# One root of a product in place of two nested roots in a hyperbolic attention, with work moved between VectorE, ScalarE and GpSimd

## The chip, the cores and the metric

The kernel runs on one core of one Trainium2 chip. The metric is the time of one execution on the device, in microseconds (us); the median of several executions is compared. PE is TensorE, DVE is VectorE, ACT is ScalarE, POOL is GpSimd, SP is SyncE.

## What is computed

The reference is one layer of a perceiver. All inputs are float32, and x has 2 batches of 256 tokens with 256 channels. Three blocks follow each other, each with a residual sum: a softmax cross attention of 16 heads to 4096 context tokens a batch, a self attention of 16 heads of 16 channels with a hyperbolic distance, and a feed-forward block of 8 experts of which each token takes the one with the highest gate. The change touches the second block only:

```
diff_sq = q_norm_sq + k_norm_sq - 2.0 * qk
denom = maximum((1.0 - q_norm_sq) * (1.0 - k_norm_sq), 1e-06)
dist = arccosh(maximum(1.0 + 2.0 * diff_sq / denom, 1.0))
attn = softmax(-dist, axis=-1)
out = einsum('bhnm,bhmd->bhnd', attn, v)
```

With r = max(diff_sq, 0) / denom, exp(-dist) can be had in two ways. The kernel before forms sqrt(2r) + sqrt(2r + 2), takes the logarithm and raises e to -2 times it. The kernel after forms sqrt(r * (r + 1)) + r, takes the logarithm of 4 times it plus 2, and raises e to -1 times it. Both give half of exp(-dist); the factor falls out of the softmax.

## The kernel before, in words

The cross attention comes first: 16 steps (8 pairs of heads by 2 batches), each over the 4096 keys. It takes most of the time. The last step (`last_step`) already has batch 0 of the second block in it: its projections, its lengths, and its 16 distance units, which DVE turns into ratios.

**The units.** The second block has 32 units m, 16 a batch, in 8 groups gg of 4 (groups 0 to 3 are batch 0, 4 to 7 are batch 1). A unit is 128 keys by 256 queries of two heads; PE leaves numerator and reciprocal denominator in two banks of PSUM (`distances`, L659 and L663), and a group is a tile of 128x2048 float32. `ratios` (L1134, L1136) has two DVE instructions a unit: the maximum with zero of the numerators, 128x512, into the group's tile, and a `scalar_tensor_tensor` that multiplies it by the smaller of 1e6 and the other half of the banks. Each batch has two pairs of banks, so PE may begin unit m only when DVE has counted up `s_rt` for unit m - 2.

**From ratios to weights.** For each group ACT takes two square roots (`root_of_product` L929 into a tile of its own, `root_of_sum` L932 in place), POOL adds them for groups 0 to 5 (L527) and DVE for 6 and 7 (L1199), ACT takes the logarithm (L944) and the exponential (L949), and PE multiplies the weights with the values (`average`, L735). Root, logarithm and exponential each need a table that is loaded when the function changes (ACT_TABLE_LOAD).

**The order after the cross attention.** It is written out by hand, an engine at a time, in `tail_dve`, `tail_act`, `tail_pe` and `tail_pool`. DVE takes the last output of the cross attention from PSUM (`take_output`, L1986), normalises it, PE turns it, ACT copies it (`take_turned_output`, L1754), PE projects it, and DVE adds it to x (`add_output`, L2004). Then come the layer norm of batch 1 (`variance`, `root_of_variance` L859, `normalised`) and its transposition (`take_batch`, L573). Then eight projections of batch 1 go round PE (`qk`, `lengths`, `norms`), ACT (`squares` L887, `rows` L896) and DVE (`low_rows` L1083), in three banks. After each, ACT's program may have one of the large operations of batch 0. Then DVE has 11 small instructions in a chain for the denominators (`inverses`, L1092 to L1108), PE places them, and ACT and DVE copy four groups each (`take_placed` L909, `take_placed_keys` L1116). Then come batch 1's 16 units, u = 0 to 15. Between them PE has the averages and turned averages of batch 0 (AVERAGE_AFTER) and turns and projects batch 0's output (`turn_output` L672, `project_output` L685), ACT copies the averages out (`take_average` L969) and the turned output (L973), and DVE has `normalise(0)` (L1183, L1187) after unit 12. DVE then adds batch 0's residual (`residual`, L1144), and the layer norm of batch 0 follows, with ACT's root L859 ahead of the logarithms and exponentials of groups 4 to 7. The experts come last.

**What waits.** An engine works through its own list in order; a wait stops all that stands behind it. In the list of ACT before, between the last rows and the layer norm of batch 0, stand in this order: logarithms 0 and 1, values 1, logarithm 2, four placed copies, logarithm 3, weights 0 to 2, average 0, weights 3, average 1, roots of group 4 with averages 2 and 3 between and behind, roots of 5 and 6, the turned output, roots of 7.

Of the kernel before, what the change touches and what calls it, by code (L numbers as in the profile page):

```python
# [20 lines left out]
ALU = mybir.AluOpType  # L21
# [69 lines left out]
BEHIND = 3  # L91
AVERAGE_AFTER = {4: (0, None), 6: (1, 0), 8: (2, 1), 9: (3, 2), 11: (None, 3)}
# [15 lines left out]
def perceiver(nc, x, ctx, wq, wk, wv, wo, aq, ak, av, ao, gw, gb, w1, b1, w2, b2, out):  # L108
# [8 lines left out]
    with stack:  # L117
# [213 lines left out]
        s_r2 = sem("s_r2")  # L331
        s_ra = sem("s_ra")
# [9 lines left out]
        s_rb = sem("s_rb")  # L342
# [175 lines left out]
        def tail_pool(pool):  # L518
# [393 lines left out]
        def tail_act(act, take_turned_output):  # L912
# [6 lines left out]

            def root_of_product(gg):  # L920

                act.wait_ge(s_rt, 8 * (gg + 1))
                if gg == 1:
                    act.wait_ge(s_el, 8)
                if gg == 2:
                    act.wait_ge(s_pv, STEPS * SLOTS)
                if gg >= 4:
                    act.wait_ge(s_ra, gg - 2)
# [6 lines left out]
            def roots(gg):  # L935
                root_of_product(gg)
                root_of_sum(gg)

            def logarithms(gg):
                if gg < 6:  # L940
                    act.wait_ge(s_ra, gg + 1)
                else:
                    act.wait_ge(s_rb, gg - 5)
                nc.scalar.activation(ratio[gg], ratio[gg], ACT.Ln).then_inc(s_lg, 1)  # L944

            def weights(gg):

                act.wait_ge(s_lg, gg + 1)
                nc.scalar.activation(ratio[gg], ratio[gg], ACT.Exp, scale=-2.0).then_inc(s_wt, 1)  # L949
# [1234 lines left out]
```

## Time and profile before

| what | value |
|---|---|
| median of 3 executions | 1107.04 us (1106.72 to 1108.7) |
| the profiled execution, its own time | 1108.32 us |
| span of the profiled execution | 1106.6 us |
| busy share of PE, DVE, ACT, POOL | 94%, 70%, 71%, 60% |
| mean granted clock of TensorE | 0.974 |
| end of PE's last matmul of the cross attention | 955.57 us of the span |

The span runs from the first to the last instruction; 1.72 us of the execution's own time lie around it. Shares are means over the whole span. A granted clock of 1.00 is full speed, 2.4 GHz, and 0.50 is 1.2 GHz. Idle time in a row is that just ahead of the instruction, and the arrow names what ended it. "xN" at a row of the timeline is N instructions merged.

### The profile page before, as it was taken

The page shows a single profiled execution, that of the slowest core. Times are in us where ns is not written, and L with a number is a line of the kernel's source. Part 1 is how long each engine was busy: PE and PEld are TensorE (multiplying, and loading weights), DVE is VectorE, ACT ScalarE, POOL GpSimd, SP SyncE. Part 2 cuts the span into 40 slices and gives each one's busy share as a digit, 9 for nine tenths or more (in the row PEclk, how much of TensorE's full clock was granted, in tenths as well). Part 3 has the DMA queues.
Part 4 walks back from the last instruction along what each step waited for, and adds up shares of the span by engine and source line. Part 5 has one row for each costly group of instructions (what it writes and reads, how often), then busy time and mean ns, then how long its engine had stood idle before and what let it go on. Part 6 is the DMA issues. An engine that isn't in the chain of part 4 may idle for free.

```text
span 1106.6 us, 36226 instructions
## 1 busy us (share of the span) xinstructions
PE 1041.5 (94%) x15401; PEld 778.4 (70%) x15401; DVE 773.8 (70%) x1061; ACT 783.3 (71%) x1197; POOL 667.0 (60%) x611
## 2 busy tenths in 40 slices
PE   6799999999999999999999999999999989667888
PEld 3376777777777777777777777777777777543566
DVE  4887877777777777777777777777767759558442
ACT  6487777777777777777777777777777756799754
POOL 6366666666666666666666666776655456833033
PEclk9999999999999999999999999999999999886699
DMA  7821330000000000000000000003000020000000
GB/s 225 238 48 26 64 55 7 17 7 16 7 16 7 17 7 16 7 17 7 17 7 17 8 16 7 16 8 121 7 2 7 9 72 3 2 1 1 1 1 20
DMA packets 50929, 31.70 MB, mean 29 GB/s; under 512 B 27194, under 2 KB 47698, under 8 KB 50770
## 3 DMA queue, kind: packets, MB, share of 16 engines
q1 hardware_dynamic: 50770, 29.39, 10.0%
q8 instruction: 123, 2.02, 0.8%
q14 instruction: 36, 0.29, 0.1%
HBM read 22.57 MB, written 0.52 MB: 21 GB/s over the span
## 4 chain that ended last, share of the span: by engine, by line
PE 82%; DVE 5%; ACT 5%; issue 4%; POOL 3%; DMA 1%; ACTq 0%; POOLq 0%; DVEq 0%
PE ps L1461 15%; PE ps L1406 14%; PE ps L1543 14%; PE ps L1490 6%; PE ps L1589 5%; PE ps L1584 5%; PE ps L1587 5%; PE ps L1531 5%; PE ps L815 2%; POOL psums L2151 2%; PE ps L775 2%; PE ps L1522 1%; PE ps L1391 1%; PE ps L591 1%; DVE m_part L1956 1%
## 5 line engine op out<-in xcount | busy, mean ns | idle before, releaser
L2151 POOL TENSOR_TENSOR psums<-probs 128x512 f16<-128x512 f32 x512 | 589.6, 1171 | 327.0 <-ACT probs L1790 270.0
L1956 DVE TENSOR_REDUCE m_part<-ps 128x2 f32<-128x1024 f32 x256 | 312.7, 1223 | 137.3 <-PE ps L1490 135.3
L1781 ACT ACTIVATE probs<-ps 128x1024 f32<-128x1024 f32 x256 | 259.8, 1015 | 200.4 <-PE ps L1543 155.4
L1790 ACT ACTIVATE probs<-probs 128x512 f16<-128x512 f32 x384 | 240.0, 627 | 4.2
L1543 PE MATMUL ps<-q_hi,k_p 64*128 64x256 f16 x2048 | 211.2, 269 | 0.0
L1584 PE MATMUL ps<-v_sb,probs 128*128 128x65 f16 x2048 | 205.1, 192 | 4.9 <-POOL psums L2151 3.6
L1587 PE MATMUL ps<-v_sb,probs 128*128 128x64 f16 x2048 | 205.0, 192 | 0.0
L1589 PE MATMUL ps<-v_sb,psums 128*128 128x65 f16 x2048 | 204.6, 194 | 0.0
L1584 PEld LDWEIGHTS ps<-v_sb,probs 128*128 128x128 f16 x2048 | 188.3, 98 | 20.0 <-POOL psums L2151 5.1
L1587 PEld LDWEIGHTS ps<-v_sb,probs 128*128 128x128 f16 x2048 | 187.9, 97 | 16.1
L1589 PEld LDWEIGHTS ps<-v_sb,psums 128*128 128x128 f16 x2048 | 188.1, 97 | 0.0
L1461 PE MATMUL ps<-wv_hi,ctx_hi 128*128 128x128 f16 x1024 | 179.4, 220 | 1.6 <-DVE v_sb L1971 1.6
L1461 PE MATMUL ps<-wv_lo,ctx_hi 128*128 128x128 f16 x1024 | 178.1, 219 | 0.0
L1461 PE MATMUL ps<-wv_hi,ctx_lo 128*128 128x128 f16 x1024 | 178.1, 219 | 0.0
L1543 PE MATMUL ps<-q_lo,k_p 64*128 64x256 f16 x1024 | 143.0, 269 | 0.0
L1947 DVE TENSOR_TENSOR k_p<-ps,k_p 128x512 f16<-128x512 f32 x124 | 85.7, 691 | 65.1 <-ACT k_p L1741 65.1
L1461 PEld LDWEIGHTS ps<-wv_hi,ctx_hi 128*128 128x128 f16 x1024 | 99.9, 98 | 40.8 <-issue 38.9
L1543 PEld LDWEIGHTS ps<-q_hi,k_p 64*128 64x128 f16 x2048 | 106.3, 94 | 19.2
L1978 DVE CAST probs<-probs 128x512 f16<-128x512 f32 x128 | 115.6, 903 | 1.5 <-ACT probs L1781 1.4
L1490 PE MATMUL ps<-k_p,q_hi 64*128 64x512 f16 x512 | 99.0, 380 | 12.3 <-DVE m_part L1956 7.1
L1531 PE MATMUL ps<-m_row,level 64*128 64x512 f16 x512 | 98.9, 376 | 1.9 <-ACT probs L1781 1.1
L1461 PEld LDWEIGHTS ps<-wv_lo,ctx_hi 128*128 128x128 f16 x1024 | 100.3, 98 | 0.1
(251 smaller groups left out, 1661.2 us busy)
## 6 DMA issues: line engine op xcount, KB each, us to landing
ctx_hi<-in_L_ffn_W_dram SPq DMA_DIRECT2D x2, 2048.0 KB, 10.3
probs<-in_ctx_dram SPq DMA_DIRECT2D x4, 512.0 KB, 7.4
wqk_raw<-in_L_xattn_w_q_dram SPq DMA_DIRECT2D x16, 128.0 KB, 2.3
wqk_raw<-in_L_xattn_w_k_dram SPq DMA_DIRECT2D x16, 128.0 KB, 2.5
k_p<-in_ctx_dram SPq DMA_DIRECT2D x4, 512.0 KB, 10.5
wv_raw<-in_L_xattn_w_v_dram SPq DMA_DIRECT2D x16, 128.0 KB, 2.5
wo_raw<-in_L_xattn_w_o_dram SPq DMA_DIRECT2D x16, 128.0 KB, 2.1
ctx_hi<-in_ctx_dram SPq DMA_DIRECT2D x7, 256.0 KB, 5.8
```

The source lines that it names most:

```text
L1406: mm = pe.matmul(ps[:, bank, :], w[:, par, c, :], y[:, b, j, c, :], start=(c == 0 and i == 0), stop=(c == 1 and i == 2))
L1461: mm = pe.matmul(ps[:, bank, t * P:(t + 1) * P], y[:, b, j, c, toks], w[:, par, c, :], start=(k == 0), stop=(k == 5))
L1490: mm = pe.matmul(ps[:, bank + 1 - h, :], q_hi[rows, n % 3, t * P:(t + 1) * P], k_p[rows, par, 0, 512 * j:512 * (j + 1)], start=True, stop= ...
L1531: pe.matmul(ps[:, score_bank(n, pair, h), :].rearrange("p (k q) -> p k q", k=2), level[rows, :], m_row[rows, n % 2, :].unsqueeze(1).to_bro ...
L1543: mm = pe.matmul(ps[:, score_bank(n, pair, h), cols], k_p[rows, par, k_part, keys], q_part[rows, n % 3, :], start=False, stop=(i == 2), sk ...
L1584: pe.matmul(out, p_hi[:, s % NP, h, queries], value[:, XD:2 * XD + 1], start=(s == 0 and h == 0 and t == 0), stop=False, skip_group_check= ...
L1587: pe.matmul(ps[:, ACC, at:at + XD], p_hi[:, s % NP, h, queries], value[:, 0:XD], start=False, stop=False, skip_group_check=True)
L1589: mm = pe.matmul(out, p_lo[:, s % NP, h, queries], value[:, XD:2 * XD + 1], start=False, stop=(s == SLOTS - 1), skip_group_check=True)
L1781: nc.scalar.activation(p_raw[:, s:s + 2, :, :].rearrange("p k h q -> p h k q"), ps[:, first:first + 2, :].rearrange("p h (k q) -> p h k q" ...
L1790: nc.scalar.activation(p_hi[:, s % NP, :, :], p_raw[:, s % NX, :, :], ACT.Copy) \
L1956: nc.vector.tensor_reduce(m_part[:, j, t, :], ps[:, bank:bank + 2, :], AX.X, ALU.max) \
L2151: nc.gpsimd.tensor_tensor(p_lo[:, s % NP, :, :].rearrange("p h q -> p (h q)"), p_raw[:, s % NX, :, :].rearrange("p h q -> p (h q)"), p_hi[ ...
```

## The change

ACT has one root for each group instead of two. DVE forms its argument, ratio times (ratio plus one), in one `scalar_tensor_tensor` of 128x2048, and adds the root to the ratio for all eight groups; POOL's six sums go. The maximum with zero of batch 1's units moves from DVE to ACT (`positive`, Relu). The logarithm takes scale 4 and a bias from a column, and stands between the rows for groups 0 to 3. Two tables of places, ROOT_AFTER and SUM_AFTER, set where groups 4 to 6 go among batch 1's units; AVERAGE_TAKEN does so for ACT's copies of the averages.

```diff
+AVERAGE_TAKEN = {5: 0, 7: 1, 9: 2, 10: 3}
+ROOT_AFTER = {5: 4, 9: 5, 13: 6}
+SUM_AFTER = {5: 4, 9: 5, 13: 6}
...
-            for gg in range(6):
-                pool.wait_ge(s_r2, gg + 1)
-                nc.gpsimd.tensor_tensor(ratio[gg], root_of(gg), ratio[gg], ALU.add) \
-                    .then_inc(s_ra, 1)
...
+            def positive(m, gg, kt, jj):
+                act.wait_ge(s_dd, m + 1)
+                if gg <= 6:
+                    act.wait_ge(s_pv, STEPS * SLOTS)
+                    act.wait_ge(s_ra, 1)
+                else:
+                    act.wait_ge(s_el, 8)
+                pair = ps[:, UNIT_BANKS[1][jj]:UNIT_BANKS[1][jj] + 2, :]
+                part = head_part(gg, kt, slice(2 * jj, 2 * jj + 2)).rearrange("p (h q) -> p h q", h=2)
+                nc.scalar.activation(part, pair[:, :, 0:TQ], ACT.Relu).then_inc(s_rl, 1)
+
             def root_of_product(gg):
...
-                nc.scalar.activation(root_of(gg), ratio[gg], ACT.Sqrt, scale=2.0)
-
-            def root_of_sum(gg):
-                nc.scalar.activation(ratio[gg], ratio[gg], ACT.Sqrt, scale=2.0,
-                                     bias=vecs[:, 2:3]).then_inc(s_r2, 1)
...
+                act.wait_ge(s_tp, gg + 1)
+                nc.scalar.activation(root_of(gg), root_of(gg), ACT.Sqrt).then_inc(s_r2, 1)
 
             def logarithms(gg):
...
-                nc.scalar.activation(ratio[gg], ratio[gg], ACT.Ln).then_inc(s_lg, 1)
+                act.wait_ge(s_ra, gg + 1)
+                nc.scalar.activation(ratio[gg], ratio[gg], ACT.Ln, scale=4.0,
+                                     bias=vecs[:, 2:3]).then_inc(s_lg, 1)
 
             def weights(gg):
...
-            roots(0)
+            root_of_product(0)
+            root_of_product(1)
             act.wait_ge(s_vone, 2)
             take_turned_output()
-            root_of_product(1)
+            root_of_product(2)
             root_of_variance(act, 2, slice(2, NT))
-            root_of_sum(1)
             take_values(0)
             take_batch(act, 1)
+            root_of_product(3)
             for i in range(9):
                 take_rows(act, i, 1)
-                if i in (1, 3):
-                    root_of_product(2 + i // 2)
-                if i in (2, 4):
-                    root_of_sum(1 + i // 2)
+                if i in (1, 3, 5, 7):
+                    logarithms(i // 2)
...
+            weights(0)
+            weights(1)
             take_values(1)
-            logarithms(2)
+            weights(2)
             for g in range(4):
                 take_placed(act, 1, g)
...
             weights(3)
...
+            for u, (m, gg, b, g, kt, jj) in enumerate(attn_units()[16:]):
+                positive(m, gg, kt, jj)
+                if u in AVERAGE_TAKEN:
+                    take_average(AVERAGE_TAKEN[u])
+                if u in ROOT_AFTER:
+                    root_of_product(ROOT_AFTER[u])
             take_turned(1, 0, OUT_BANKS[0][0])
-            roots(7)
+            root_of_product(7)
             root_of_variance(act, 3, slice(0, 2))
             for gg in range(4, 8):
                 logarithms(gg)
...
+            if b == 1:
+                dve.wait_ge(s_rl, m - 15)
+                nc.vector.scalar_tensor_tensor(part, pair[:, :, TQ:2 * TQ], 1e6, part,
+                                               ALU.min, ALU.mult).then_inc(s_rt, 2)
+                return
...
+        def product(dve, gg):
+            dve.wait_ge(s_rt, 8 * (gg + 1))
...
+            nc.vector.scalar_tensor_tensor(root_of(gg), ratio[gg], 1.0, ratio[gg], ALU.add, ALU.mult) \
+                .then_inc(s_tp, 1)
+
+        def sum_of_roots(dve, gg):
+            dve.wait_ge(s_r2, gg + 1)
+            nc.vector.tensor_tensor(ratio[gg], root_of(gg), ratio[gg], ALU.add).then_inc(s_ra, 1)
...
             variance(2, slice(2, NT))
             normalised(2, slice(2, NT))
+            product(dve, 3)
+            sum_of_roots(dve, 0)
             for i in range(8):
                 low_rows(dve, i, 1)
+                if i in (0, 2, 4):
+                    sum_of_roots(dve, 1 + i // 2)
...
             for u, (m, gg, b, g, kt, jj) in enumerate(attn_units()[16:]):
                 ratios(dve, m, gg, b, kt, jj)
+                if u % 4 == 3:
+                    product(dve, gg)
+                if u in SUM_AFTER:
+                    sum_of_roots(dve, SUM_AFTER[u])
                 if u == NORMALISE_AFTER:
                     normalise(0)
...
-            sum_of_roots(6)
             residual(0)
             variance(3, slice(0, 2))
             normalised(3, slice(0, 2))
-            sum_of_roots(7)
+            sum_of_roots(dve, 7)
...
             last_step(STEPS - 1)
+            for gg in range(2):
+                product(dve, gg)
             take_output(STEPS - 1, STEPS * SLOTS - 1)
             normalise(STEPS - 1)
+            product(dve, 2)
             add_output(STEPS - 1, 1)
```

## Rows read from the trace of the kernel before

**Rows 1.** The page: span and instructions, and the shares of the chain by engine.
```profile
span 1106.6 us, 36226 instructions
...
PE 82%; DVE 5%; ACT 5%; issue 4%; POOL 3%; DMA 1%; ACTq 0%; POOLq 0%; DVEq 0%
```

**Rows 2.** The chain that ended last, 1015 to 1024 us: start, us, what.
```profile
1015.64 0.59 ACT xnT L973
...
1016.27 3.80 PE ps L685 x8
...
1020.09 0.70 DVE x_sb L1144
...
1022.31 1.28 ACT L944
```

**Rows 3.** Busy time by stretch; after POOL the granted clock, DMA share, GB/s.
```profile
950.00:966.00 16.00, 9.88 (x68) 7.10 (x69) 5.87 (x17) 11.84 (x13) 12.04 (x14) 0.68 0.01 2
966.00:982.00 16.00, 14.65 (x66) 11.64 (x65) 3.38 (x7) 13.23 (x20) 11.44 (x3) 1.00 0.00 1
...
993.00:1018.00 25.00, 19.23 (x192) 9.55 (x193) 22.60 (x37) 23.75 (x19) 9.04 (x2) 0.70 0.00 1
```

**Rows 4.** Groups by line, ScalarE, 930 to 1107 us: busy, mean ns, idle before.
```profile
L932 ACT ACTIVATE k_p<-k_p,vecs 128x2048 f32<-128x2048 f32 x4 | 8.0, 1994 | 0.0
L944 ACT ACTIVATE k_p<-k_p 128x2048 f32<-128x2048 f32 x4 | 7.5, 1902 | 0.0
...
L944 ACT ACT_TABLE_LOAD x2 | 2.6, 1283 | 0.0
...
L973 ACT ACTIVATE xnT<-ps 128x512 f32<-128x512 f32 x2 | 1.2, 590 | 1.7 <-PE ps L672 1.7
```

**Rows 5.** Two lines side by side, VectorE and GpSimd: ns min/median/max.
```profile
L880 DVE SCALAR_TENSOR_TENSOR ctx_hi<-ctx_hi x4: 1212/1598/2177, 938.9 to 949.3; 128x1024 f16<-128x1024 f32 x4
...
L2151 POOL TENSOR_TENSOR psums<-probs x14: 1154/1159/2145, 931.4 to 953.5; 128x512 f16<-128x512 f32 x14
```

**Rows 6.** VectorE in order of time: start us, us, instruction, idle before it.
```profile
955.61 0.43 DVE L1986 COPY o_acc<-ps 128x264 f32<-128x264 f32 x1 [4.18 <-PE ps L1589]
...
960.15 0.69 DVE L2004 TENSOR_TENSOR x_sb<-x_sb,ps 128x512 f32<-128x512 f32 x1 [3.44 <-PE ps L1522]
...
982.45 0.41 DVE L1092 TENSOR_SCALAR last_raw<-ps 128x256 f32<-128x256 f32 x1
...
992.99 0.69 DVE L1134 TENSOR_SCALAR v_sb<-ps 128x512 f32<-128x512 f32 x1 [1.17 <-PE ps L663]
...
1012.65 0.76 DVE L1187 TENSOR_TENSOR xn<-ps,orec 128x256 f32<-128x256 f32 x2
...
1016.68 0.69 DVE L1136 SCALAR_TENSOR_TENSOR ctx_hi<-ps,ctx_hi 128x512 f32<-128x512 f32 x1
1017.29 2.28 DVE L1199 TENSOR_TENSOR ctx_lo<-probs,ctx_lo 128x2048 f32<-128x2048 f32 x1
```

**Rows 7.** ScalarE in order of time: start us, us, instruction, idle before it.
```profile
957.60 0.38 ACT L1754 ACTIVATE o_turn<-ps 128x256 f32<-128x256 f32 x1 [1.12 <-POOL psums L523]
...
966.81 0.38 ACT L887 ACTIVATE ctx_lo<-ps 128x256 f32<-128x256 f32 x1 [1.22 <-PE ps L591]
...
981.54 0.47 ACT L896 ACTIVATE spare<-ps,vecs 128x256 f16<-128x256 f32 x1 [0.39 <-PE ps L601]
...
991.36 0.38 ACT L909 ACTIVATE wqk_raw<-ps 128x256 bf16<-128x256 f32 x1 [0.26 <-PE ps L637]
...
1022.09 0.20 ACT L859 ACTIVATE rstd<-var 128x2 f32<-128x2 f32 x1 [0.88 <-DVE var L1900]
```

**Rows 8.** TensorE in order of time, inside the stretch of batch 1's units.
```profile
994.46 0.82 PE L659 MATMUL ps<-spare 32*128 32x256 f16 x6 [1.48 <-DVE v_sb L1136]
...
998.07 1.93 PE L735 MATMUL ps<-k_p,psums 128*32 128x256 f32 x16
...
1004.35 1.07 PE L735 MATMUL ps<-k_p,psums 128*32 128x256 f32 x16
```

More of the change, by code:

```diff
@@ L331, in perceiver @@
         s_r2 = sem("s_r2")
+        s_tp = sem("s_tp")
+        s_rl = sem("s_rl")
         s_ra = sem("s_ra")
@@ L341, in perceiver @@
         s_ge = sem("s_ge")
-        s_rb = sem("s_rb")
         s_bt = sem("s_bt")
@@ L918, in take_values @@
                                          ACT.Copy).then_inc(s_vx, 1)
-            def root_of_product(gg):
[L922 to L928, printed above, removed]
-                nc.scalar.activation(root_of(gg), ratio[gg], ACT.Sqrt, scale=2.0)
-            def root_of_sum(gg):
-                nc.scalar.activation(ratio[gg], ratio[gg], ACT.Sqrt, scale=2.0,
-                                     bias=vecs[:, 2:3]).then_inc(s_r2, 1)
@@ L935, in roots @@
-            def roots(gg):
-                root_of_product(gg)
-                root_of_sum(gg)
-            def logarithms(gg):
[L940 to L943, printed above, removed]
-                nc.scalar.activation(ratio[gg], ratio[gg], ACT.Ln).then_inc(s_lg, 1)
+            def positive(m, gg, kt, jj):
[8 more added lines that the diff above has]
+                nc.scalar.activation(part, pair[:, :, 0:TQ], ACT.Relu).then_inc(s_rl, 1)
@@ L946, in weights @@
+            def root_of_product(gg):
+                act.wait_ge(s_tp, gg + 1)
+                nc.scalar.activation(root_of(gg), root_of(gg), ACT.Sqrt).then_inc(s_r2, 1)
+            def logarithms(gg):
+                act.wait_ge(s_ra, gg + 1)
+                nc.scalar.activation(ratio[gg], ratio[gg], ACT.Ln, scale=4.0,
+                                     bias=vecs[:, 2:3]).then_inc(s_lg, 1)
             def weights(gg):
                 act.wait_ge(s_lg, gg + 1)
-                nc.scalar.activation(ratio[gg], ratio[gg], ACT.Exp, scale=-2.0).then_inc(s_wt, 1)
@@ L951, in tail_act @@
-            roots(0)
+                nc.scalar.activation(ratio[gg], ratio[gg], ACT.Exp, scale=-1.0).then_inc(s_wt, 1)
+            root_of_product(0)
+            root_of_product(1)
             act.wait_ge(s_vone, 2)
             take_turned_output()
-            root_of_product(1)
+            root_of_product(2)
             root_of_variance(act, 2, slice(2, NT))
-            root_of_sum(1)
             take_values(0)
             take_batch(act, 1)
+            root_of_product(3)
             for i in range(9):
@@ L975, in take_turned @@
                     .then_inc(s_xc, 1)
-            for gg in range(2):
-                logarithms(gg)
+            weights(0)
+            weights(1)
             take_values(1)
-            logarithms(2)
+            weights(2)
             for g in range(4):
                 take_placed(act, 1, g)
-            logarithms(3)
-            weights(0)
-            weights(1)
-            weights(2)
-            take_average(0)
-            weights(3)
-            take_average(1)
-            root_of_product(4)
-            take_average(2)
-            root_of_sum(4)
-            take_average(3)
-            roots(5)
-            roots(6)
+            weights(3)
+            for u, (m, gg, b, g, kt, jj) in enumerate(attn_units()[16:]):
[4 more added lines that the diff above has]
+                    root_of_product(ROOT_AFTER[u])
             take_turned(1, 0, OUT_BANKS[0][0])
-            roots(7)
+            root_of_product(7)
             root_of_variance(act, 3, slice(0, 2))
@@ L1137, in ratios @@
                                            ALU.min, ALU.mult).then_inc(s_rt, 1)
+        def product(dve, gg):
+            dve.wait_ge(s_rt, 8 * (gg + 1))
+            if gg == 0:
+                dve.wait_ge(s_sc, STEPS * PAIRS_A_STEP)
+            if gg == 1:
+                dve.wait_ge(s_el, 8)
+            if gg == 2:
+                dve.wait_ge(s_pv, STEPS * SLOTS)
+            if gg >= 4:
+                dve.wait_ge(s_ra, gg - 2)
+            nc.vector.scalar_tensor_tensor(root_of(gg), ratio[gg], 1.0, ratio[gg], ALU.add, ALU.mult) \
[3 more added lines that the diff above has]
+            nc.vector.tensor_tensor(ratio[gg], root_of(gg), ratio[gg], ALU.add).then_inc(s_ra, 1)
         def tail_dve(dve, variance, normalised):
@@ L1193, in tail_dve @@
                 ratios(dve, m, gg, b, kt, jj)
+                if u % 4 == 3:
+                    product(dve, gg)
+                if u in SUM_AFTER:
+                    sum_of_roots(dve, SUM_AFTER[u])
                 if u == NORMALISE_AFTER:
                     normalise(0)
-            def sum_of_roots(gg):
-                dve.wait_ge(s_r2, gg + 1)
-                nc.vector.tensor_tensor(ratio[gg], root_of(gg), ratio[gg], ALU.add).then_inc(s_rb, 1)
-            sum_of_roots(6)
             residual(0)
```

## The prediction

> **What bounds the kernel now.** The page comes first: a span of 1106.6 us, whose last chain is PE for 82% [rows 1]. Nearly all of that is the cross attention, which the change leaves alone until its last microseconds. So I read the chain in order of time behind it. From 1015.64 us it runs: ACT copies the turned output (0.59), PE projects it (3.80), DVE adds it (0.70), and at 1022.31 ACT loads the table for logarithms 4 to 7 [rows 2]. From there ACT's own list sets the pace up to the experts, and the change leaves that list's order as it is. What is late at ACT's small root of the layer norm (L859, 1022.09) is therefore late at the end. This instruction is my finish line.
>
> Busy time by stretch says who is near the limit ahead of it. In the 25 us of batch 1's units DVE is busy 22.60 us and ACT 23.75 [rows 3]: two engines, both nearly full. Between 966 and 982 PE is busy 14.65 us of 16 at a granted clock of 1.00, 2.4 GHz, and DVE 3.38; from 950 to 966 DVE is busy 5.87. So ACT has no room among the units, and neither has DVE; DVE has much room before them.
>
> **Times are told from two marks.** c is the time since DVE takes the cross attention's last output (955.61 before) [rows 6]. Before, in c: ACT's turned copy 1.99, first square 11.20, last rows end 26.40, last placed copy ends 36.13, root of the layer norm 66.48 [rows 7]; add_output 4.54, first inverse 26.84, first ratio 37.38, last ratio's start 61.07 [rows 6].
>
> **Prices.** A root, logarithm or exponential of 128x2048 takes 1.90, with a bias column 1.99, a table load 1.28 [rows 4]; in a row each starts some 0.1 before the last ends, so I count 1.8. A sum on DVE takes 2.28, the multiplying half of a ratio 0.69, started back to back every 0.66 or so [rows 6]. The product is not in the trace. Its nearest rows are the sum of the same shape, 2.28, and the same operation on half the elements, 1.21 alone and 2.18 beside GpSimd [rows 5]. I take 2.28 and, beside GpSimd, 4.1; the lower bound is half, 1.14. Relu is not there either. A copy of its shape out of PSUM takes 0.59 [rows 4], and I take that; DVE's maximum of the same shape takes 0.69 [rows 6], the upper bound.
>
> **Step 1, products 0 and 1 ahead of take_output.** DVE's list ends at 951.4 and DVE is idle for the 4.18 us before 955.61 [rows 6]. Two products alone would end at 956.0. But GpSimd still has the last splits of the probabilities to do, and one of these takes 1.16 alone and up to 2.14 beside a DVE instruction with two inputs [rows 5]. Product 0 runs beside them all, to 955.5; the splits end near 956.7 instead of 954.7; product 1 ends near 958.4. Mark c starts **2.8 us late**. Bounds: 0.4 if neither slows the other, 4.0 if product 1 is slowed to its end. Behind these products on DVE's list stands take_output, and behind that PE, ACT and the whole block. Root 1 on ACT ends just as the turned output is ready (c = 2.0), so it adds nothing.
>
> **Step 2, product 2, product 3, sum 0.** Product 2 fits into the 3.44 us in which DVE waits for the projection [rows 6]. Product 3 follows the normalised rows at c = 8.6 and ends at 10.9; root 3 follows it to 12.8, and ACT's first square stands behind it: 12.8 instead of 11.2. Next to be late is PE's first length.
>
> **Step 3, the rows.** Before, four large operations stood between them and they took 15.2 us [rows 7]. Now four logarithms stand there and the table load is among them, 1.28 more; before it came after the last row, under DVE's inverses. Following the list, I find that ACT waits for PE less: last rows end at 27.6, 14.8 after the first square. Sums 1 to 3 (2.28 each) fit under the logarithms. The inverses start at c = 28.05, **1.2 us late**. By the Trainium skill, "ScalarE: Activation LUTs", section "What ACT_TABLE_LOAD costs", a switch of tables costs about 2.66 us, as a drain follows the load. In the trace the load takes 1.28 and the next operation follows at once [rows 4]; by the page the forecast would be about 1.4 us later.
>
> **Step 4, up to the first unit.** The inverses take 5.9 as before. ACT's load and weights 0 to 2 take their place under them, as the logarithms did, to c = 35.0, when the first placed bank is there. Placed copies end at 37.35. But now weights 3 (1.9) stands ahead of the first unit's maximum, where before DVE began on its own: the maximum starts at 39.25. GpSimd's six sums cost nothing before (it was idle otherwise) and their going gains nothing.
>
> **Step 5, the 16 units.** DVE had 32 instructions of 0.66 and 1.1 for normalise: 24.3 us from 992.99 to 1017.29 [rows 6]. Now it has 16 (10.6), four products (9.1), three sums (6.8) and normalise: **27.6**, even without a wait. And it waits. PE starts unit u + 2 only when DVE has done unit u, and needs 1.05 a unit at 1.2 GHz (granted 0.50), with 1.93 for an average at that clock and 1.07 at the higher [rows 8]; before, DVE had 1.32 of work on the other pair of banks to cover this, now 0.66. With U counted from the first maximum:
> - units 0 to 3: PE brings unit 2 at 2.5 and unit 3, which must wait for ratio 1, at 3.5; product 4 ends at 7.1.
> - units 4 to 7: average 0 on PE holds up unit 5 (8.5). ACT then has average 0's copy, a table load and root 4, to 12.05, and DVE's sum 4 waits for it: 2.9 idle. Sum 4 to 14.4, units 6 and 7, product 5 to 17.95.
> - units 8 to 11: averages 2 on PE and 2's copy and root 5 on ACT hold up sum 5 (21.1 to 23.4); product 6 ends at 27.0.
> - units 12 to 15: normalise, unit 13, sum 6 to 31.7, unit 15 to 33.0, product 7 to 35.3.
> - ACT copies the turned output at 31.5 to 32.1, PE projects for 3.8 [rows 2], residual at 35.9, finish line 2.0 later at 37.9. I take 38.
> With PE at 1.2 GHz throughout, it is 39.5; where it is at 2.4 GHz almost throughout, 35.3. The clock averaged 0.70 before [rows 3].
>
> **Step 6, behind the line.** Logarithms 4 to 7 gain the bias column, 0.09 each: 0.4. The roots that ACT is spared, eight of 1.9, and the 16 maxima it takes on, cancel only on ACT; they were not what it ends up waiting for.
>
> **The sum.** Finish line at c = 39.25 + 38 = 77.25 instead of 66.48: 10.8. With 2.8 of step 1 and 0.4 of step 6: **14.0 us slower**. The profiled execution took 1108.32 (span 1106.6 and 1.7 around it), so 1122.3; it lies 1.3 over the median of 1107.04, so against the median **1121 us**. A measurement of this kernel can tell 0.2%, 2.2 us, from no change. The forecast's own ends: 0.4 in step 1, the fast clock and a Relu a little shorter give 1116; 4.0 in step 1, the slow clock and 2 us of rows at half clock give 1126.
>
> **Rivals.**
> - *The waits hide.* ACT and PE run ahead while DVE does its products, and sums 4 to 6 never wait. DVE then works for 27.6 us from U = 0.6; the finish line is at c = 39.25 + 30.2 = 69.5, so 3.0 + 2.8 + 0.4 = 6.2: 1113, or 1111 with 0.4 in step 1. For it: before, DVE was idle for under 3 us of 25. Against: root 4 stands behind maximum 5 and a table load, and sum 4 straight behind unit 5. Chance 0.14.
> - *Faster: ACT's list alone decides.* The chain names it, and from the last placed copy to the turned output it had 23.9 us; now weights 3, 16 maxima at 0.5, four averages' copies, one load and three roots make 18.1, 5.8 less. For DVE to keep out of the way its products and sums would have to run at half their price, 1.14, so that its 27.6 become 19.6; from about 1.7 each the gain is gone. Time: -5.8, with 0.4, 1.2 and 0.4 of the other steps, is -3.8: 1103. Against: the sum of this shape has 2.28. Chance 0.04.
> - *PE's clock stays at 1.2 GHz through the rows.* Longer gaps ahead of them (ACT's root 3, the later output) would do it. PE's work of some 1.7 us a row then doubles, about 13 us more: 1134. Against: the clock was 0.68 on average in the stretch ahead, with PE busy 9.88 of 16 us, and rose all the same [rows 3], and what PE does just ahead is the same. Chance 0.06.
> - *The tables do not fit.* If the logarithm's table lacks the square, or the root's lacks Relu, each change between them costs a load: six more in the rows, 7.7 us, 1129. For it: squares stood only beside roots and exponentials so far. The Trainium skill, "ScalarE: Activation LUTs", section "Table sets: the hidden batching unit", has relu and copy in every set, and does not name the square there; the trace shows copies beside all three without a load. Chance 0.05.
> - *No change*, DVE's extra work and ACT's relief cancelling within 2.2 us: 1107. Chance 0.03; nothing but luck speaks for it.
>
> **How the numbers follow.** The forecast keeps 0.68. The range of 1111 to 1126 takes in it and the hidden waits, 0.82, and leaves out the slow rows, the tables, no change and faster. Slower by over 0.2%: 0.93; within: 0.03; faster: 0.04.
>
> **What would show it.** Right: DVE busy some 28 us between first ratio and last product with idle of 6 to 9 us, most of it ahead of sum 4 and for ACT's Relu; take_output 2 to 3 us later, with GpSimd's last splits at 2 us; one table load among the rows; the first maximum behind weights 3; the finish line near 1036. Wrong: products well under 2 us, sums 4 to 6 that start without idle time, or more than six loads from the root's on to the last exponential's.

## The result, and the profile after

| | before | after |
|---|---|---|
| median of 4 executions | 1107.40 us (1106.72 to 1108.7) | 1122.51 us (1122.19 to 1125.46) |
| profiled execution, its own time | 1108.32 us | 1122.19 us |
| its span | 1106.6 us | 1120.5 us |
| mean granted clock | 0.974 | 0.968 |
| ratio of after to before | | 1.0136, 95% interval 1.0121 to 1.0152 |

The change makes the kernel 15.1 us slower by the medians; 1121 was predicted, with a range of 1111 to 1126. First the page of the kernel after, its lines to be read beside [rows 1]:

```profile
span 1120.5 us, 36259 instructions
...
PE 1041.9 (93%) x15401; PEld 778.7 (70%) x15401; DVE 796.0 (71%) x1059; ACT 778.5 (69%) x1205; POOL 644.0 (57%) x605
...
PE 81%; DVE 6%; issue 5%; ACT 5%; POOL 3%; DMA 0%; DVEq 0%; ACTq 0%; POOLq 0%
```

PE's share of the chain is smaller by a point and DVE's larger by one, and the span is 13.9 us longer. Busy time by stretch of the kernel after, columns as in [rows 3]; the last row is from 18 us behind the finish line to the end, and a row of the kernel before for the same stretch follows in a fence of its own:

```profile
950.00:966.00 16.00, 7.68 (x54) 5.85 (x51) 12.28 (x15) 8.16 (x8) 9.16 (x11) 0.61 0.01 2
966.00:982.00 16.00, 12.37 (x54) 9.27 (x54) 12.46 (x16) 12.78 (x19) 0.00 (x0) 0.97 0.00 1
998.00:1037.00 39.00, 25.12 (x201) 11.92 (x197) 28.39 (x31) 19.91 (x27) 0.00 (x0) 0.61 0.00 1
1055.00:1121.00 66.00, 56.30 (x447) 43.09 (x446) 23.86 (x66) 33.75 (x77) 21.38 (x32) 0.97 0.03 9
```

```profile
1040.00:1107.00 67.00, 58.29 (x452) 44.42 (x448) 24.06 (x66) 32.99 (x75) 21.34 (x32) 0.95 0.03 9
```

From 950 to 966 DVE is busy 12.28 us instead of 5.87, and the granted clock is 0.61 instead of 0.68. Through the rows the clock is 0.97. The stage of the units is now 39 us long, at a clock of 0.61, and DVE is busy for 28.39 of them. VectorE of the kernel after in order of time (start us, us, instruction, idle before it):

```profile
950.55 3.24 DVE L1141 SCALAR_TENSOR_TENSOR k_p<-k_p 128x2048 f32<-128x2048 f32 x1
953.71 3.24 DVE L1141 SCALAR_TENSOR_TENSOR ctx_hi<-k_p 128x2048 f32<-128x2048 f32 x1
958.89 0.43 DVE L1998 COPY o_acc<-ps 128x264 f32<-128x264 f32 x1 [1.94 <-PE ps L1601]
...
963.43 0.69 DVE L2016 TENSOR_TENSOR x_sb<-x_sb,ps 128x512 f32<-128x512 f32 x1 [1.24 <-PE ps L1534]
...
987.65 0.41 DVE L1079 TENSOR_SCALAR last_raw<-ps 128x256 f32<-128x256 f32 x1
...
999.36 1.29 DVE L1123 SCALAR_TENSOR_TENSOR v_sb<-ps,v_sb 128x512 f32<-128x512 f32 x2 [2.35 <-ACT v_sb L929]
1001.90 1.29 DVE L1123 SCALAR_TENSOR_TENSOR v_sb<-ps,v_sb 128x512 f32<-128x512 f32 x2 [1.26 <-ACT v_sb L929]
...
1007.28 0.69 DVE L1123 SCALAR_TENSOR_TENSOR k_p<-ps,k_p 128x512 f32<-128x512 f32 x1 [1.16 <-PE ps L663]
1010.68 2.29 DVE L1146 TENSOR_TENSOR v_sb<-ctx_hi,v_sb 128x2048 f32<-128x2048 f32 x1 [2.71 <-ACT ctx_hi L933]
...
1018.88 0.69 DVE L1123 SCALAR_TENSOR_TENSOR ctx_lo<-ps,ctx_lo 128x512 f32<-128x512 f32 x1 [1.78 <-ACT ctx_lo L929]
1020.86 2.29 DVE L1146 TENSOR_TENSOR k_p<-probs,k_p 128x2048 f32<-128x2048 f32 x1 [1.28 <-ACT probs L933]
...
1032.37 2.29 DVE L1141 SCALAR_TENSOR_TENSOR ctx_hi<-ctx_hi 128x2048 f32<-128x2048 f32 x1
1035.47 0.69 DVE L1153 TENSOR_TENSOR x_sb<-x_sb,ps 128x512 f32<-128x512 f32 x1 [0.81 <-PE ps L685]
```

The last L880 ahead of these rows starts at 948.45 and takes 2.17. Behind product 1 DVE waits 1.94 us for PE. Among the units it waits six times for ACT or PE, 1.26 + 1.16 + 2.71 + 1.78 + 1.28 + 0.81 = 9.0 us. ScalarE of the kernel after, same columns:

```profile
956.98 1.91 ACT L933 ACTIVATE ctx_hi<-ctx_hi 128x2048 f32<-128x2048 f32 x1 [1.25 <-DVE ctx_hi L1141]
...
971.51 0.64 ACT L887 ACTIVATE ctx_lo<-ps 128x256 f32<-128x256 f32 x2
...
973.16 1.28 ACT L937 ACT_TABLE_LOAD   x1
974.46 2.00 ACT L937 ACTIVATE k_p<-k_p,vecs 128x2048 f32<-128x2048 f32 x1
...
986.75 0.46 ACT L896 ACTIVATE spare<-ps,vecs 128x256 f16<-128x256 f32 x1
...
996.83 1.90 ACT L943 ACTIVATE ctx_lo<-ctx_lo 128x2048 f32<-128x2048 f32 x1
998.63 1.08 ACT L929 ACTIVATE v_sb<-ps 128x512 f32<-128x512 f32 x2
...
1018.16 0.60 ACT L929 ACTIVATE ctx_lo<-ps 128x512 f32<-128x512 f32 x1 [2.85 <-PE ps L663]
...
1037.46 0.20 ACT L859 ACTIVATE rstd<-var 128x2 f32<-128x2 f32 x1 [0.86 <-DVE var L1912]
```

The finish line (L859) is at 1037.46. The whole way, from three marks (the end of DVE's last L880, take_output, the finish line):

| stretch | before | after | difference | predicted |
|---|---|---|---|---|
| end of L880 to take_output | 951.43 to 955.61: 4.18 | 950.62 to 958.89: 8.27 | +4.1 | +2.8 |
| take_output to first ratio or Relu of batch 1 | 37.38 | 39.74 | +2.4 | +1.9 |
| from there to the finish line | 29.10 | 38.83 | +9.7 | +8.9 |
| finish line to the end of the span | 84.51 | 83.04 | -1.5 | +0.4 |

The four differences are 14.7 us; the cross attention ended 0.8 earlier in this profile (950.62 against 951.43), which leaves the 13.9 us between the spans. That end moves from one profile to the next whatever the edit behind it: in the runs below the last L880 ends anywhere from 948.99 to 953.89. So stretches are compared from their own marks. The stretch behind the finish line moves too, with nothing changed in it (see step 6 at the end).

### The profile page after: what moved, and what is told of

Its sections match the earlier page's. It is cut to its first block, busy times and chain, and to the rows that moved or that the text cites. A ratio compares the mean times of both kernels' runs of the same rounds, so it can differ in the third digit from the quotient of the medians.

```text
span 1120.5 us, 36259 instructions
## 1 busy us (share of the span) xinstructions
PE 1041.9 (93%) x15401; PEld 778.7 (70%) x15401; DVE 796.0 (71%) x1059; ACT 778.5 (69%) x1205; POOL 644.0 (57%) x605
## 4 chain that ended last, share of the span: by engine, by line
PE 81%; DVE 6%; issue 5%; ACT 5%; POOL 3%; DMA 0%; DVEq 0%; ACTq 0%; POOLq 0%
PE ps L1473 15%; PE ps L1418 14%; PE ps L1555 14%; PE ps L1502 6%; PE ps L1601 5%; PE ps L1596 5%; PE ps L1599 5%; PE ps L1543 5%; POOL psums L2166 2%; PE ps L815 2%; PE ps L775 2%; PE ps L1534 1%; PE ps L1403 1%; DVE m_part L1968 1%; PE ps L591 1%
## 6 DMA issues: line engine op xcount, KB each, us to landing
k_p<-in_ctx_dram SPq DMA_DIRECT2D x4, 512.0 KB, 10.6
```

## The experiments

Unless said otherwise an experiment is the kernel after with one edit, and its difference is told against after's 1122.51. The kernel before ran beside each and had 1107.4 to 1107.5. "Behind the line" is from the finish line to the end of the span.

### Step 1: is it the two products, and is it GpSimd?

**The products left out.** ACT's roots 0 and 1 take the ratio itself.

```diff
-            for gg in range(2):
-                product(dve, gg)
             take_output(STEPS - 1, STEPS * SLOTS - 1)
```

> The kernel after, with products 0 and 1 left out (the roots of groups 0 and 1 are taken of the ratio itself, so r instead of r times r plus 1 goes into them). Contention theory: the last splits on GpSimd go back from above 3 us to about 1.2 each while VectorE is idle, the take of the last output comes 3.3 to 4 us earlier against the first instruction, and all of that reaches the end: 3 to 4 us less than the kernel after, some 1118.5 to 1119.5 us. Rival, that the delay is caught up before the finish line (rows bound by ScalarE's own list): less than 1 us.

Measured: 1119.44 us, ratio 1.0109 (1.0094 to 1.0124), 3.1 less than after. VectorE in order of time:

```profile
951.72 2.17 DVE L880 SCALAR_TENSOR_TENSOR ctx_hi<-ctx_hi 128x1024 f16<-128x1024 f32 x1
958.07 0.43 DVE L2003 COPY o_acc<-ps 128x264 f32<-128x264 f32 x1 [4.18 <-PE ps L1606]
```

From the end of L880 (951.72 + 2.17 = 953.89) to take_output it is 4.18 us again, to the hundredth as before the change; the finish line comes 82.79 us behind the end of L880 instead of 86.84. So the products cost 4.1 us on the way to take_output, just over the upper bound of 4.0.

They cost it in a way that I had not costed. Product 0 takes 3.24, not 4.1, and so does product 1, so DVE's list ends at 956.95; it is the splits that end late. GpSimd's line in the kernel after (ns min/median/max), beside [rows 5]:

```profile
L2166 POOL TENSOR_TENSOR psums<-probs x10: 1148/1942/3202, 938.5 to 954.8; 128x512 f16<-128x512 f32 x10
```

and the chain that ended last (start, us, what):

```profile
951.60 6.37 POOL psums L2166 x2
```

A split takes up to 3.20 us instead of 2.14, and the last two end at 957.97, where the kernel before had them done at 954.68. Two readings fit: both engines run at about half rate while they overlap, or they take turns, an instruction at a time. By turns, the longest split is its own 1.15 plus most of a product's 2.28, and a product is 2.28 plus the rest of a split. Cutting each product into four tells them apart, since a turn then is short.

```diff
+        def product_piece(dve, gg, piece):
...
+            k, cols = piece // 2, slice(piece % 2 * 512, piece % 2 * 512 + 512)
+            i = nc.vector.scalar_tensor_tensor(root_of(gg)[:, k, cols], ratio[gg][:, k, cols], 1.0,
+                                               ratio[gg][:, k, cols], ALU.add, ALU.mult)
...
-                product(dve, gg)
+                for piece in range(4):
+                    product_piece(dve, gg, piece)
```

> The kernel after, with products 0 and 1 each cut in four instructions of 128x512. Theory: an instruction of VectorE with two inputs in SBUF and one of GpSimd take turns, whole instructions at a time. Then a split waits for one piece, not for a whole product: 1.2 plus 0.6, some 1.8 us instead of 3.2, the last split ends 2 us earlier, and pieces beside splits take up to 1.8 us, later ones 0.7; VectorE's list, 8.3 us of pieces and waits, then sets the take: within 1 us of the kernel after. Rival, both run at once at about half their rate: splits near 2.1 to 3.2 as they are, pieces at 1.2 to 1.3 each.

Measured: 1121.98 us, ratio 1.0129 (1.0113 to 1.0144), 0.5 less, which this measurement can't tell from nothing. The pieces of products 0 and 1 (ns min/median/max), and GpSimd's last seven splits:

```profile
L1149 DVE SCALAR_TENSOR_TENSOR k_p<-k_p x4: 678/1531/1636, 951.7 to 956.2; 128x512 f32<-128x512 f32 x4
L1149 DVE SCALAR_TENSOR_TENSOR ctx_hi<-k_p x4: 677/678/679, 956.8 to 958.6; 128x512 f32<-128x512 f32 x4
```

```profile
943.90 11.79 POOL L2177 TENSOR_TENSOR psums<-probs 128x512 f16<-128x512 f32 x7 [0.36 <-DVE probs L2000]
```

A piece alone takes 0.68, beside a split 1.53 to 1.64: its own time plus most of a split's 1.15, where half rate would have given it 1.2 to 1.3. A split takes 11.79 / 7 = 1.68 us, where the same seven took 15.02 / 7 = 2.15 in the kernel after. GpSimd is done 4.1 us behind the end of L880 (943.90 + 11.79 = 955.69, less 951.55) instead of 7.35. Now DVE's own list holds take_output: it starts at 959.17 with no idle time ahead of it, 7.6 behind that end. **Turns it is**, and the time hardly moves because what one engine gains the other loses.

The Trainium skill has this rule: "SBUF — State Buffer", section "SBUF: two separate sides", calls the pair of ports that VectorE and GpSimd share an exclusive lock: of a VectorE instruction with two inputs in SBUF and a GpSimd instruction that reads SBUF, whichever starts first holds it for its whole length, and the other is blocked. The runs agree, with 3.20 us for a split behind a product and 1.53 for a piece behind a split; [rows 5] had shown it, and I had read the 2.14 there as a rate.

**The products behind take_output and the normalisation**, with their roots behind the turned output:

```diff
-            for gg in range(2):
-                product(dve, gg)
             take_output(STEPS - 1, STEPS * SLOTS - 1)
             normalise(STEPS - 1)
-            product(dve, 2)
+            for gg in range(3):
+                product(dve, gg)
```

> The kernel after, with products 0 and 1 behind the take and the normalisation of the last output. The splits on GpSimd go back to 1.2 us and the take comes 4.1 us earlier after the last expert weights' split, but three products (6.9 us) stand ahead of the addition of the output, for which 3.4 us were free: 0 to 1.5 us less than the kernel after. Rival, that only the place ahead of the take costs: 3 us less, as with these products left out.

Measured: 1123.59 us, ratio 1.0142 (1.0128 to 1.0157), 1.1 more, with overlapping intervals.

VectorE in order of time:

```profile
955.57 0.43 DVE L1998 COPY o_acc<-ps 128x264 f32<-128x264 f32 x1 [4.17 <-PE ps L1601]
...
963.20 0.68 DVE L2016 TENSOR_TENSOR x_sb<-x_sb,ps 128x512 f32<-128x512 f32 x1
```

take_output comes 4.17 us behind L880 again, but add_output waits for three products, 7.63 us behind take_output instead of 4.54. Finish line behind the end of L880: 86.97, against 86.84. The gain is all given back: of the two places tried, neither is free for two products.

### GpSimd again: the sums

```diff
+            for gg in range(7):
+                pool.wait_ge(s_r2, gg + 1)
+                nc.gpsimd.tensor_tensor(ratio[gg], root_of(gg), ratio[gg], ALU.add).then_inc(s_ra, 1)
...
-            sum_of_roots(dve, 0)
...
-                if u in SUM_AFTER:
-                    sum_of_roots(dve, SUM_AFTER[u])
```

> The kernel after, with sums 0 to 6 back on GpSimd (4.5 us each), VectorE only sum 7. Theory of VectorE's work and its waits for the roots: the stretch of the units loses three sums (6.8 us) and the waits ahead of them (4 us), of which PE's averages and ScalarE's roots keep some: 6 to 8 us less than the kernel after, 1114.5 to 1116.5. Rival, the round trips bind and not VectorE's work: 0 to 3 us less.

Measured: 1132.33 us, ratio 1.0223 (1.0208 to 1.0238), **9.8 more**. Both theories fell. VectorE in order of time, and GpSimd beside it:

```profile
961.81 0.69 DVE L2015 TENSOR_TENSOR x_sb<-x_sb,ps 128x512 f32<-128x512 f32 x1 [1.24 <-PE ps L1533]
...
965.52 3.91 DVE L1920 TENSOR_TENSOR newton<-rstd 128x2 f32<-128x2 f32 x1
969.46 4.42 DVE L1921 TENSOR_TENSOR newton<-newton,var 128x2 f32<-128x2 f32 x1
...
974.31 0.73 DVE L1925 TENSOR_SCALAR xn<-x_sb,mv,rstd 128x256 f32<-128x256 f32 x2
...
1020.89 4.81 DVE L1144 SCALAR_TENSOR_TENSOR probs<-k_p 128x2048 f32<-128x2048 f32 x1
...
1029.75 4.64 DVE L1144 SCALAR_TENSOR_TENSOR probs<-ctx_lo 128x2048 f32<-128x2048 f32 x1
...
1039.69 3.39 DVE L1144 SCALAR_TENSOR_TENSOR ctx_hi<-ctx_hi 128x2048 f32<-128x2048 f32 x1
```

```profile
964.91 4.50 POOL L531 TENSOR_TENSOR k_p<-ctx_hi,k_p 128x2048 f32<-128x2048 f32 x1
969.36 4.50 POOL L531 TENSOR_TENSOR k_p<-probs,k_p 128x2048 f32<-128x2048 f32 x1
```

The layer norm's instructions on 128x2 take 0.16 us alone, but the first `tensor_tensor` of them waits out sum 1 (to 969.41) and the next the whole of sum 2 (to 973.86): 3.91 and 4.42. From add_output to the normalised rows it is 12.50 us (961.81 to 974.31) instead of 3.30 in the kernel after; that is 9.2 of the 9.9 by which the first Relu comes later behind take_output (49.66 us for 39.74). The kernel before had the same sums on GpSimd and paid nothing at this place, by luck: its small instructions of this layer norm ran from 961.95 to 963.41, and the sums beside it from 956.80 to 961.32 and from 964.32. Among the units DVE is rid of three sums, 6.9 us, and the stage is only 0.6 shorter (first Relu 1006.92, finish line 1045.18: 38.3). That doesn't show that DVE's work is no bound: products 5, 6 and 7 now wait for GpSimd's sums and take 4.81, 4.64 and 3.39 us instead of 2.29, which gives back 6.0 of the 6.9. This run can't answer the question of step 5; the next ones do.

### Step 5: work or waits?

**Maxima back on DVE** (`ratios` with both halves for batch 1, no `positive`):

```diff
-                positive(m, gg, kt, jj)
...
-                dve.wait_ge(s_rl, m - 15)
...
-                return
```

> The kernel after, with the maxima of batch 1 back on VectorE; products, sums and order as after. Theory of VectorE's work: 16 more instructions of 0.66 on the busiest engine of the stretch, 10.6 us, of which the present idle time (some 9 us, most of it waits for ScalarE's Relu) takes up 6 to 8: 2 to 5 us slower than the kernel after. Rival, the round trip over a third engine is what costs: the stretch becomes 3 us or more shorter than after.

Measured: 1126.35 us, ratio 1.0167 (1.0152 to 1.0183), 3.8 more. From the first ratio (999.74) to the finish line (1040.36) 40.6 us, almost without idle time on DVE, while ACT waits 6.73 for the last product. Against the 38.83 of the kernel after that is 1.8 more for 10.6 us of DVE's work; the other 2 us lie outside the units, 1.5 of them behind the line (84.54 us for 83.04, with the same work there). Once products and sums are on DVE, giving the maxima to ACT helps, by about 1.8 us, and the rival, that the trip over ACT costs more than it saves, is out.

**Sums two units later**, so that their roots are long done:

```diff
-SUM_AFTER = {5: 4, 9: 5, 13: 6}
+SUM_AFTER = {7: 4, 11: 5, 15: 6}
```

> The kernel after, with VectorE's sums 4, 5, 6 two units later (after units 7, 11, 15), ScalarE's order unchanged. Theory: VectorE waited 2.7 and 1.3 us for roots 4 and 5; now units 6 and 7 fill that time, and sum 6 leaves the path to the last unit: 2 to 4 us less than after. Rival, TensorE's averages and the round trips would have held the units up anyway: within 1 us.

Measured: 1123.55 us, ratio 1.0144 (1.0127 to 1.0161), 1.0 more, with overlapping intervals: the rival.

VectorE in order of time:

```profile
1012.01 1.29 DVE L1123 SCALAR_TENSOR_TENSOR k_p<-ps,k_p 128x512 f32<-128x512 f32 x2 [3.29 <-ACT k_p L929]
```

Sum 4 (1015.54) no longer waits, but DVE then waits 3.29 us at unit 6, for ACT's Relu, where it had waited 2.71 for the root: ACT's list has the root ahead of this Relu, and PE behind both. Sum 6 ends just ahead of the residual (1036.49) and delays it by 0.9: PE was done at 1035.55.

**No products and no sums among the units** (products 4 to 7, sums 4 to 6):

```diff
-                if u % 4 == 3:
-                    product(dve, gg)
-                if u in SUM_AFTER:
-                    sum_of_roots(dve, SUM_AFTER[u])
```

> The kernel after, with products 4 to 7 and sums 4 to 6 left out (roots 4 to 7 are taken of the ratio itself, and logarithms 4 to 6 of the ratio without its root). It takes 15.9 us of work from VectorE in the stretch of the units and leaves each unit's round trip TensorE, ScalarE, VectorE. Theory of VectorE's work: the stretch is bound by it, 10 us or more less than the kernel after, 1112 or below. Rival, the round trip with the averages on TensorE (16 units at 1.05, averages and turns 10 us at 1.2 GHz) binds at some 27 us: 4 to 7 us less, 1115.5 to 1118.5.

Measured: 1116.98 us, ratio 1.0078 (1.0061 to 1.0096), 5.5 less: the rival.

VectorE in order of time:

```profile
1014.03 1.29 DVE L1127 SCALAR_TENSOR_TENSOR k_p<-ps,k_p 128x512 f32<-128x512 f32 x2 [3.29 <-ACT k_p L929]
```

Seven instructions of 2.2, some 15 us of DVE's work, are gone, and only 5.1 us of time: from the first Relu (1001.39) to the finish line (1035.09) it is 33.7 us instead of 38.83. Even so it is 4.6 longer than before's 29.10. What is left is the trip PE, ACT's Relu, DVE, PE, with the averages and roots in ACT's list between the Relus; the 3.29 us above are for a Relu that stands behind a table load and root 4. No run takes the roots out of that list, so how much the trip alone costs and how much the roots in it isn't told apart. Outside the units the rows come 1.3 us later and the stretch behind the line is 1.7 shorter (81.31), with the same work as in the kernel after; step 6 below says what goes with that.

**Batch 0 as after, batch 1 as before** (two roots, sums 4 and 5 on GpSimd, maxima on DVE):

```diff
-                positive(m, gg, kt, jj)
...
+            old_root(4)
+            take_average(2)
+            old_root_of_sum(4)
...
+            for gg in range(4, 6):
+                pool.wait_ge(s_r2, gg + 1)
+                nc.gpsimd.tensor_tensor(ratio[gg], root_of(gg), ratio[gg], ALU.add).then_inc(s_ra, 1)
```

> Batch 0 as in the kernel after (one root, products and sums 0 to 3 on VectorE, logarithms between the rows), batch 1 as in the kernel before (two roots, maxima on VectorE, sums 4 and 5 on GpSimd). Theory: the two halves of the change add up. Batch 0's half keeps the 4 us at the take of the last output and 1 to 2 us of rows, 5 to 6 us over before, 1112.5 to 1113.5; the units take their old 24 to 25 us. Rival, batch 0's half is the whole loss because the units then start with ScalarE behind: over 1118; or it is none of it: under 1109.

Measured: 1112.14 us, ratio 1.0044 (1.0029 to 1.0058). By the medians batch 0's half of the change costs 4.7 us, and what is left for batch 1's half is 10.4. take_output is 8.27 behind L880 as in the kernel after, and the units have 28.86 us (998.38 to 1027.24), before's 29.10: batch 0's half doesn't reach into them. By the marks its share is larger: from the end of L880 (949.49) to the finish line it is 77.75 us, for 70.66 before and 86.84 after, so 7.1 of 16.2. Of these 7.1, 1.3 are a later first row at a low clock, which two other profiles with this code have and the kernel after's has not. No run has batch 1's half alone, so that the halves add up is seen from this side only.

### Is there a version that gains?

**The kernel before, with one root for groups 4 and 5 only**, their product on GpSimd, which has room, and four of their maxima on ACT:

```diff
+ONE_ROOT = (4, 5)
+MAXIMA_BY_ACT = (8, 9, 10, 11)
...
+            def pool_product(gg):
...
+                nc.gpsimd.tensor_scalar(root_of(gg), ratio[gg], 1.0, None, ALU.add).then_inc(s_tp, 1)
...
+                nc.gpsimd.tensor_tensor(root_of(gg), root_of(gg), ratio[gg], ALU.mult) \
```

> The kernel before, with one root for groups 4 and 5 only: their products (an addition and a multiplication) and their sums on GpSimd, which is idle there; ScalarE takes over the maxima of units 8 to 11 in place of the two roots it is spared; sum 6 behind the layer norm. VectorE's units read one operand from PSUM and so keep clear of GpSimd. Theory: VectorE loses 2.6 us in the stretch and the finish line comes 1 to 2 us earlier than before, 1105.5 to 1106.5. Rival: the round trip over ScalarE costs what the maxima save, or GpSimd's long instructions hold up VectorE's small ones of the layer norm as in the run with its sums on GpSimd: same or up to 4 us slower.

Measured: 1112.17 us, ratio to before 1.0039 (1.0025 to 1.0052), 4.7 slower than before.

VectorE and GpSimd of this kernel in order of time:

```profile
1007.09 0.69 DVE L1174 SCALAR_TENSOR_TENSOR ctx_lo<-ps,ctx_lo 128x512 f32<-128x512 f32 x1 [1.22 <-ACT ctx_lo L966]
1011.00 1.45 DVE L1174 SCALAR_TENSOR_TENSOR ctx_lo<-ps,ctx_lo 128x512 f32<-128x512 f32 x2 [3.23 <-ACT ctx_lo L966]
...
1023.27 4.11 DVE L1943 TENSOR_SCALAR var<-mv 128x2 f32<-128x2 f32 x1
```

```profile
1008.41 5.36 POOL L536 TENSOR_SCALAR probs<-k_p 128x2048 f32<-128x2048 f32 x1
...
1022.85 4.50 POOL L531 TENSOR_TENSOR k_p<-probs,k_p 128x2048 f32<-128x2048 f32 x1
```

The same trap: `variance` of batch 0, 0.17 us, waits 4.11 for a sum on GpSimd, and the finish line is 3.9 later for it. The four Relus cost DVE 1.22 and 3.23 of waiting besides.

**The kernel before, with the turned output one place earlier.** ACT copies it ahead of the second root of group 6 and not behind it, and DVE has sum 6 behind the layer norm. Nothing of the change is in it.

```diff
-            roots(6)
+            root_of_product(6)
             take_turned(1, 0, OUT_BANKS[0][0])
+            root_of_sum(6)
...
-            sum_of_roots(6)
             residual(0)
             variance(3, slice(0, 2))
             normalised(3, slice(0, 2))
+            sum_of_roots(6)
```

> The kernel before, with ScalarE's copy of the turned output ahead of root of sum 6 and VectorE's sum 6 behind the layer norm. Theory: the copy is 1 us late behind that root, but TensorE's last unit ends 0.5 us ahead of the projection's present start, so the finish line comes 0.4 us earlier: same as before within the noise, ratio 0.9996. Rival: roots of group 7 and sum 6 become late instead, 1 to 2 us slower.

Measured: 1106.29 us over 11 executions, ratio to before 0.9984 (0.9975 to 0.9993). It is the only version here that beats both kernels: the one before by 1.1 us by the medians (1107.42 beside it) and 1.8 by the ratio, more than the 0.4 expected.

ScalarE in order of time:

```profile
1015.03 0.60 ACT L973 ACTIVATE xnT<-ps 128x512 f32<-128x512 f32 x1 [0.15 <-PE ps L672]
...
1021.98 0.20 ACT L859 ACTIVATE rstd<-var 128x2 f32<-128x2 f32 x1 [0.35 <-DVE var L1901]
```

The finish line comes 69.98 us behind the end of L880 (952.00) instead of 70.66, 0.7 less. That much the edit explains: the copy no longer waits for the root (it starts at 1015.03, straight behind PE), and the projection then waits for PE's last unit, which waited for DVE. The rest is behind the line, 82.82 us for 84.51, where the profile has a granted clock of 0.97 from 1040 to 1105 against 0.95; this stretch moves by more than that from profile to profile, and whether the edit has a part in it stays open.

## Why the prediction was right, and where it was off

**Bound, right.** The finish line at L859 carried the argument: what came late there came late at the end, but for 1.5 us.

**Step 1, mis-sized: 4.1 instead of 2.8, outside its own bounds.** The mechanism (products against GpSimd's last splits, and PE behind these) was right, the run without them shows. The term failed at "product 0 ... to 955.5" beside GpSimd at 4.1 and splits at up to 2.14. I took both numbers of [rows 5], 2.14 and 2.18, for rates. They hold a wait: a split waits until DVE's instruction is over, so behind a product of 2.28 it takes 3.20, and a product behind a split takes 3.24. The total was then set by GpSimd and not, as forecast, by product 1.

**Step 2, right.** Product 2 hides under the projection (add_output at c = 4.54, as before), root 1 ends at 958.89, with take_output; the first square comes at c = 12.62 for 12.8.

**Step 3, right to 0.7.** Last rows end at c = 28.32 for 27.6, inverses at 28.76 for 28.05. One load stands among the rows, and by it the difference between row and page is settled: it takes 1.28 us and the logarithm starts at 974.46, 1.30 behind the load's start, so the 1.4 us more of the page's rule do not come here.

**Step 4, right.** The last placed copy ends at c = 38.04 for 37.35, and weights 3 (996.83) stands ahead of the first Relu, at 39.74 for 39.25: most of step 3's 0.7 carried along.

**Step 5, right to 0.8.** In U, from the first Relu (998.63): product 4 ends at 6.9 (7.1 forecast), sum 4 starts at 12.05 (12.05), product 5 ends at 17.9 (17.95), sum 5 starts at 22.2 (21.1), sum 6 ends at 32.5 (31.7), product 7 at 36.0 (35.3), the finish line is at 38.8 (38). The one step that failed is sum 5's: DVE waited 1.78 us for the Relu of unit 9, which ACT could begin only at 1018.16, after 2.85 us of waiting for PE. PE in order of time shows what stood ahead of unit 9:

```profile
1014.60 1.94 PE L735 MATMUL ps<-k_p,psums 128*32 128x256 f32 x16
1016.46 0.69 PE L746 MATMUL ps<-ident,ctx_lo 128*128 128x128 f32 x2
1017.08 0.82 PE L659 MATMUL ps<-spare 32*128 32x256 f16 x6
```

An average at 1.2 GHz (1.94), which I had, and the turning of another (0.69), which I had not counted: 0.7 of the 1.1 by which sum 5 was late. All that follows keeps about 0.8 of it.

**Step 6, wrong in sign.** Behind the line it took 1.5 us less where 0.4 more was forecast. The four logarithms did cost 0.09 each (1.99 for 1.90), and with batch 1 as before, where logarithms 4 to 7 are those of the kernel before, it was 83.16 us, so they are not the cause. The granted clock is what goes with it. The experiments that leave the work behind the line as in the kernel after took from 81.31 us (no products and sums among the units) to 84.54 (maxima on DVE) there, with granted clocks of 1.00 and 0.95 from 18 us behind the line to the end; the kernel after had 83.04 at 0.97, the kernel before 84.51 at 0.95. So the 1.5 us lie inside what this stretch moves by with its work unchanged. What makes the clock fall there is open. The 1.9 us between forecast and measurement here, and the 0.8 by which the cross attention ended early in this profile, cover the 1.3 of step 1 and the 1.3 of steps 3 to 5: the spans differ by 13.9 for a forecast of 14.0. That agreement is luck, and the median, 1.5 us over 1121, is nearer than the terms deserve.

**The rivals.** *The waits hide* is refuted twice: DVE was idle for 9.0 us, and taking away some 15 us of its work brought only 5.1. My 27.6 us of work were right as a sum and not the bound: with 10.6 us more of it, maxima back on DVE, the stage was 1.8 longer. *ACT's list alone decides* fell with the price of a product, 2.28. *PE's clock through the rows* did not come in the kernel after (0.97). In three experiments (maxima on DVE, no products and sums, batch 1 as before) the clock was 0.57 from 8 to 16 us behind take_output, for 0.99 in the kernel after, and the first table load came 1.3 to 1.4 us later: the effect is there, at a tenth of the 13 us. *The tables* did not come; squares ran among the logarithms without a load.

## What to carry to other kernels

Price an instruction of VectorE with two inputs in SBUF, beside a busy GpSimd, at its own time plus what is left of GpSimd's instruction, and GpSimd's at its own plus VectorE's; look above all for the tiny instructions on the critical path (0.16 us became 4.4), and place GpSimd's long ones away from them, or cut them. An operation moved from one engine to another in the middle of a producer's round (PE, ACT, DVE, PE, with two buffers) adds its wait to every round, and the freed engine's time is worth little then (10.6 us of maxima moved for 1.8, 15 us of products and sums left out for 5.1): count rounds as well as busy time. Compare stretches from marks of their own before you explain a difference of 1 or 2 us: here the last stretch moved by 3.2 us with its work unchanged. Before an operation is replaced, ask which of the operations spared was on the chain: sixteen roots became eight here. The chain of the kernel before ran through ACT's roots among the units, yet a root of 2 us moved out of the way brought only 0.7, since PE and DVE stood right behind it. A chain names what ended last and not how close the next one is.

## What the runs showed of the hardware that I had not expected

- What an instruction of VectorE with two inputs in SBUF loses is what is left of GpSimd's, whatever its own size. With the sums on GpSimd, instructions of 128x2 started 3.89 and 4.40 us ahead of a sum's end and took 3.75 and 4.26 more than their 0.16; products of 128x2048 started 2.66, 2.49 and 1.24 ahead of one and took 2.52, 2.35 and 1.10 more than their 2.29. In every one of these the wait is what was left less 0.14. A `tensor_scalar` of 128x2 waited too (4.11), though it has one input; the Trainium skill's same section counts operations in a mode with two ports among those that take the lock, and no run here shows the mode.
- Instructions of VectorE with one input in SBUF and the other in PSUM did not wait: a ratio beside GpSimd's product (1007.09, with one root for groups 4 and 5) kept its 0.69. The reciprocal of 128x2, with one input, kept its 0.17 beside a sum (965.32, with the sums on GpSimd).
- GpSimd's `tensor_scalar` of 128x2048 float32 took 5.36 and 5.37 us, more than its sum of two such tiles, 4.50 to 4.55.
- Relu of 128x512 out of PSUM took 0.60 us on ScalarE and its maximum on VectorE 0.68: for this shape the two prices are close.
